# Cross attention after self attention: the order of projection tiles, peaks, scores and the last turn in the second norm, and the order of work at the program's entry

## The reference, cut to what matters

```python
x = x + attention(layer_norm(x, g1, b1), layer_norm(x, g1, b1), wq1, wk1, wv1, wo1, bo1)
x = x + attention(layer_norm(x, g2, b2), context, wq2, wk2, wv2, wo2, bo2)
x = x + geglu_ff(layer_norm(x, g3, b3), w_ff1, b_ff1, w_ff2, b_ff2)
# attention: softmax(q k^T / 8) v per head, then @ wo + bo
# layer_norm: (x - mean) * rsqrt(var + 1e-5) * g + b
```

## Time and profile before

| | us |
|---|---|
| median of 3 runs | 2185.67 |
| lowest and highest | 2182.62 and 2186.26 |
| the profiled execution, its own time | 2181.03 |
| its span, first to last instruction | 2179.3 |

### The profile page before, as it was taken

The page is one execution under the profiler, slowest core; times in us unless marked ns, Lnnn a source line. Parts: engine busy times, 40 slices in busy tenths (PEclk is TensorE's granted clock), DMA queues, the critical chain, the costliest instruction groups (busy, mean ns, idle before and its releaser), DMA issues.

```text
span 2179.3 us, 58920 instructions
## 1 busy us (share of the span) xinstructions
PE 2087.8 (96%) x25120; PEld 1411.8 (65%) x25120; DVE 1622.4 (74%) x3014; ACT 1474.3 (68%) x1950; POOL 1379.3 (63%) x860
## 2 busy tenths in 40 slices
PE   5999999899999999989999999999999999999999
PEld 2666666675666666667466666676746666667675
DVE  5888887557588888665768888866576888885664
ACT  3888889245488888834548888873355888886342
POOL 5878887263378887725347887863434888775450
PEclk8999999999999999999999999999999999999999
DMA  4322320031332232004032233100403323210030
GB/s 129 82 57 64 73 71 19 11 72 49 76 91 65 58 87 53 29 6 99 25 93 74 64 78 75 45 29 6 99 18 93 84 69 84 55 38 21 18 67 20
DMA packets 134245, 127.82 MB, mean 59 GB/s; under 512 B 83424, under 2 KB 95712, under 8 KB 133984
## 3 DMA queue, kind: packets, MB, share of 16 engines
q1 hardware_dynamic: 133744, 123.67, 22.4%
q10 hardware_dynamic: 240, 0.39, 0.1%
HBM read 55.72 MB, written 4.19 MB: 27 GB/s over the span
## 4 chain that ended last, share of the span: by engine, by line
PE 75%; DVE 9%; ACT 5%; POOL 5%; issue 3%; DMA 1%; POOLq 1%; SPq 1%; DVEq 0%; ACTq 0%
PE work L976 10%; PE scores L1000 9%; PE scores L993 9%; PE scores L890 6%; PE scores L892 5%; PE scores L891 5%; PE work L1022 5%; PE work L1018 5%; PE work L1020 5%; PE work L890 4%; PE work L892 4%; PE work L891 4%; DVE minima L1564 2%; ACT prob L1364 1%; PE work L1030 1%
## 5 line engine op out<-in xcount | busy, mean ns | idle before, releaser
L826 POOL TENSOR_TENSOR prob<-prob 128x1024 f16<-128x1024 f32 x328 | 709.0, 2178 | 297.6 <-ACT prob L1364 281.6
L1564 DVE TENSOR_REDUCE minima<-work 128x1 f32<-128x512 f32 x1024 | 681.8, 684 | 53.6 <-PE work L976 47.8
L1363 ACT ACTIVATE prob<-scores 128x1024 f32<-128x1024 f32 x512 | 526.4, 1028 | 93.6 <-PE scores L1000 73.9
L1364 ACT ACTIVATE prob<-scores 128x1024 f16<-128x1024 f32 x512 | 522.8, 1021 | 0.0
L1018 PE MATMUL work<-vals,prob 128*128 128x65 f16 x4096 | 428.8, 192 | 2.2 <-POOL prob L826 1.8
L1022 PE MATMUL work<-vals,prob 128*128 128x65 f16 x4096 | 429.5, 195 | 0.0
L1020 PE MATMUL work<-vals,prob 128*128 128x64 f16 x4096 | 429.2, 193 | 0.0
L1018 PEld LDWEIGHTS work<-vals,prob 128*128 128x128 f16 x4096 | 383.0, 99 | 66.1 <-issue 17.9
L976 PE MATMUL work<-ka,qa 128*128 128x512 f16 x1024 | 390.0, 384 | 28.1 <-DVE minima L1564 19.2
L1020 PEld LDWEIGHTS work<-vals,prob 128*128 128x128 f16 x4096 | 379.8, 97 | 52.8
L1022 PEld LDWEIGHTS work<-vals,prob 128*128 128x128 f16 x4096 | 380.2, 97 | 0.0
(11 more groups left out here) (168 smaller groups left out, 4169.3 us busy)
## 6 DMA issues: line engine op xcount, KB each, us to landing
qa<-staged_q SPq DMA_DIRECT2D x128, 128.0 KB, 2.3
ka<-staged_k SPq DMA_DIRECT2D x126, 128.0 KB, 2.3
raw_even<-in_pairs SPq DMA_DIRECT2D x32, 384.0 KB, 3.4
raw_odd<-in_pairs SPq DMA_DIRECT2D x32, 384.0 KB, 3.4
raw_odd<-in_pieces SPq DMA_DIRECT2D x20, 512.0 KB, 3.3
raw_even<-in_pieces SPq DMA_DIRECT2D x20, 512.0 KB, 3.5
qb<-staged_q SPq DMA_DIRECT2D x64, 128.0 KB, 2.3
kb<-staged_k SPq DMA_DIRECT2D x63, 128.0 KB, 2.3
```

Of the source, the lines that this page charges most:

```text
L826: pool.tensor_tensor(prob[1][:, slot, :], prob32[:, slot, :], prob[0][:, slot, :], ALU.subtract).then_inc(a.polished, 1)
L1363: act.activation(prob32[:, n % RING, :], source, ACT.Exp)
L1364: act.activation(prob[0][:, n % RING, :], source, ACT.Exp)\
L1564: dve.tensor_reduce(minima[:, t, h:h + 1], out[:, :], AX.X, ALU.max, negate=True)\
```

## The change

In the second norm PE does project 6 right behind project 5, then the six peaks of tiles 0 and 1, project 7, turn 2, the six peaks of tiles 2 and 3, and goes to the scores. Shift 0 stands inside score 0, turn 3 behind score 0. The later peaks are spread over four scores (2, 4, 4, 2, places in `X_LATER_AT`), and shift 1 is beside score 4. DVE's list follows: normalise 2 ahead of the first peaks, moments 3 ahead of the second six, normalise 3 behind all twelve, then shift 0 and split 2; split 3 stands ahead of the first peak of step 2. ACT's and POOL's lists for this stage are unchanged.

At the entry, `attention(0)` on SP begins before the bias rows, S1 and W0 are fetched; these come behind the moves of head 1. ACT issues the key moves of head 0 rather than of head 1. DVE does two moments, two normalises, two moments, the low part of the weights, then normalise 2, split 0, normalise 3 and the other splits.

```diff
+X_LATER_AT = {0: (2, 3), 1: (0, 1, 2, 3), 2: (0, 1, 2, 3), 3: (0, 2)}
+X_LATER_STEPS = max(X_LATER_AT)
...
@@ SP, spread @@
+                    if opening and which == "k":
+                        for part in "qk":
+                            for dest, source in moves(part, step.par, 1):
+                                sp.dma_start(dest, source).then_inc(a.head1_ready, 16)
+                        load_rows(0)
+                        fetch(0, "S", 1)
+                        fetch(0, "W", 0)
+                        return
...
-                    if which == "k" and opening:
-                        for dest, source in moves("q", step.par, 1):
-                            sp.dma_start(dest, source).then_inc(a.head1_ready, 16)
...
-            load_rows(0)
-            fetch(0, "S", 1)
-            fetch(0, "W", 0)
...
@@ PE, cross @@
                 project(index, 5, 0)
-                for p in range(2):
-                    for t in (2 * p, 2 * p + 1):
-                        for group in range(len(PEAK_GROUPS)):
-                            peak(t, group)
-                    project(index, p + 6, 0)
+                project(index, 6, 0)
+                for t in range(2):
+                    for group in range(len(PEAK_GROUPS)):
+                        peak(t, group)
+                project(index, 7, 0)
                 turn(index + 1, 2)
-                shift(0)
-                turn(index + 1, 3)
+                for t in range(2, HALF):
+                    for group in range(len(PEAK_GROUPS)):
+                        peak(t, group)
+                later = iter(X_LATER)
                 for n in range(X_ALL):
                     beside = {}
-                    if n < 3:
-                        beside = {k: (peak, at) for k, at in enumerate(X_LATER[4 * n:4 * n + 4])}
-                    elif n == 3:
+                    if n == 0:
+                        beside[1] = shift, (0,)
+                    elif n == X_LATER_STEPS + 1:
                         beside[0] = shift, (1,)
+                    if n == 1:
+                        turn(index + 1, 3)
+                    for k in X_LATER_AT.get(n, ()):
+                        beside[k] = peak, next(later)
                     score(n, beside)
...
@@ ACT, entry @@
-            for dest, source in moves("k", 0, 1):
-                act.dma_start(dest, source).then_inc(a.head1_ready, 16)
+            for dest, source in moves("k", 0, 0):
+                act.dma_start(dest, source).then_inc(a.head0_ready, 16)
...
@@ DVE, cross @@
                 split(index + 1, 1)
-                for t in range(2):
-                    for group in range(len(PEAK_GROUPS)):
-                        peak(t, group)
                 take_y(index, 6)
                 normalise(index + 1, 2)
-                for t in range(2, HALF):
+                for t in range(2):
                     for group in range(len(PEAK_GROUPS)):
                         peak(t, group)
                 take_y(index, 7)
                 moments_of(index + 1, 3)
+                for t in range(2, HALF):
+                    for group in range(len(PEAK_GROUPS)):
+                        peak(t, group)
+                normalise(index + 1, 3)
                 shift(0)
-                normalise(index + 1, 3)
                 split(index + 1, 2)
-                split(index + 1, 3)
+                later = iter(X_LATER)
                 for n in range(X_ALL):
-                    if n < 3:
-                        for at in X_LATER[4 * n:4 * n + 4]:
-                            peak(*at)
-                    elif n == 3:
+                    for at in X_LATER_AT.get(n, ()):
+                        if n == 2 and at == 0:
+                            split(index + 1, 3)
+                        peak(*next(later))
+                    if n == X_LATER_STEPS + 1:
                         shift(1)
...
@@ DVE, entry @@
-            for p in range(GROUPS):
+            for p in range(2):
                 hold(dve, first_loaded[p], 16)
                 moments(0, p)
...
+            normalise(0, 0)
+            normalise(0, 1)
+            for p in range(2, GROUPS):
+                hold(dve, first_loaded[p], 16)
+                moments(0, p)
+            dve.wait_ge(first_weights, 1)
...
+            normalise(0, 2)
+            split(0, 0)
+            normalise(0, 3)
+            for p in range(1, GROUPS):
+                split(0, p)
```

More of the change, by code:

```diff
@@ L1800, in feed_forward @@
                             ahead(name)
-            for p in range(GROUPS):
+            for p in range(2):
                 hold(dve, first_loaded[p], 16)
                 moments(0, p)
[L1805 to L1817, removed]
+            normalise(0, 0)
[4 more added lines that the diff above has]
+            dve.wait_ge(first_weights, 1)
+            high, low = [wp["S"][:, part, :, :].rearrange("p s n -> p (s n)") for part in range(2)]
+            dve.scalar_tensor_tensor(out=low, in0=raw[0][:, 0:6 * P], scalar=W_SCALE, in1=high,
+                                     op0=ALU.mult, op1=ALU.subtract).then_inc(raw_used[0], 1)
+            dve.drain().then_inc(self_split, 1)
+            normalise(0, 2)
[3 more added lines that the diff above has]
+                split(0, p)
             hold(dve, params_loaded, 16)
```

## The result

| | before | changed |
|---|---|---|
| median, us (first comparison, 4 runs each) | 2185.48 | 2159.39 |
| lowest and highest | 2182.62, 2186.26 | 2157.23, 2162.83 |
| ratio, 95% interval | | 0.9883 [0.9872, 0.9895] |
| the profiled execution, its own time | 2181.03 | 2162.83 |
| its span | 2179.3 | 2161.1 |

The changed kernel is 26.1 us faster by the medians; 2163.4 had been forecast. The two profiled executions differ by only 18.2 us: that of before was among the fastest of its kernel and that of the changed kernel the slowest of its four. Why is a point of its own further down.

A forecast was written before the change was run, and what follows sets the result against it. TensorE's own work plus its gaps was taken as the bound. 18.0 us from four rounds and 4.3 from the entry gave 22.3, so 2158.7 against the profiled 2181.03 and a median of 2163.4; range 2154 to 2174.

The forecast's parts named there:

- What bounds the kernel: Whole kernel: TensorE, busy in 96% of the span, sets the length by its own work plus its gaps.
- Part 1: New order in each of four rounds: TensorE's waits fall from 8.7 to 4.2 us, gaining 4.5 per round, 18.0 in four.
- Exponential 0 behind norm 3: ScalarE in each round: norm 3 now precedes exponential 0, done at 422.65; score 2 wants to start at 423.56; cost nothing.
- slower rival: In the rounds, VectorE reaching normalise 3 over 3.7 us late adds time; slower from 9.3 us of lateness; chance 0.04.
- Part 2: Program entry, once: first maximum 6.8 us earlier, but 2.3 us of new wait for S1's split; gain 4.3 us.
- the 28.1 of the shared engines: Entry: time in us when eight key moves in line from 23.8 are through, at 0.54 us each on shared DMA engines.
- the 27.2 of issue time alone: Entry: earliest start of the maxima, in us, if only the issue time of the key moves counted.
- The clock: Entry: TensorE's clock may stay full after a shorter pause; value taken 0, bound +1.2 us.
- The total: Whole kernel: 18.0 from the rounds plus 4.3 from the entry, 22.3 us; forecast median 2163.4.
- S1 does not gate the entry: Rival at the entry: no gating by S1 and the clock stays full; entry gain 8.0, 2159.7 us; chance 0.14.
- Half was not given back: Rival in the rounds: half given back, waits of 6.5 and gain 2.2 per round; 2172.5 us; chance 0.16.
- Nothing gained: Rival: turn waits return at the shift inside score 0 and S1 undoes the entry's key moves; about 2185 us; chance 0.04.

## Why the prediction was right, point by point

- *What bounds the kernel.* PE's work and its gaps. Right: the work stayed (2087.8 and 2087.5 us), and the gaps removed by the change showed in the end.
- *Part 1, the laid-out order.* 4.5 us a round had been worked out; 4.63 was measured. The waits came at the places named: before peaks 5 and 11 (0.45 and 0.43 laid out, 0.36 and 0.35 listed), the shift (0.45, 0.23), the second later peak (0.35, 0.16), and the one that got worse, in score 2 (0.95, 0.82). Score 0's closing pair is 6.2 us earlier against projection 5, as said (15.82 against 22.06).
- *Exponential 0 behind norm 3.* It was said to cost nothing, with 0.9 us of slack. ACT in the changed kernel, the end of norm 3 and the two exponentials of score 0:

```profile
417.92 0.57 ACT L1392 ACTIVATE t<-work,params 128x256 f32<-128x256 f32 x1
418.37 1.03 ACT L1423 ACTIVATE prob<-scores 124x1024 f32<-124x1024 f32 x1
419.27 1.04 ACT L1424 ACTIVATE prob<-scores 124x1024 f16<-124x1024 f32 x1
```

  They end at 420.31, and score 2 starts at 421.37 right behind score 1, with no wait: 1.06 us of slack. The slower rival's condition was never near.
- *Part 2, the entry.* The mechanism was right, S1's fetch behind the moves, with PE waiting for POOL's split behind the ninth maximum. Its size was not: 4.3 had been forecast and 2.1 came. Three terms fell short. The nine moves went out at 0.70 us each rather than 0.645, so S1 was issued at 29.58 and not 29.0. S1 reached POOL after 5.2 us and not 4.0. The 4.0 was taken from a fetch at the head of the line; this one had the rows ahead of it. With both the projections start at 38.26, 2.5 us earlier than before (40.79) instead of 4.3. The third term is the clock, below. The first maximum, at 28.94 and not 28.0 because the last key move took 4.0 us to land and not 3.1, cost nothing, as S1 came later. Window 26 to 28 us of the changed kernel:

```profile
26.00:28.00 2.00, 0.00 (x0) 0.00 (x0) 1.29 (x2) 0.91 (x2) 0.55 (x1) 1.00 1.02 264
```

  The DMA engines are full from 26 to 34 us. The moves' latency was taken from a stretch with one queue at work, though the share of 0.81 for three moves alone stood in the rows. The rule of the Trainium skill (Trainium Kernel Development and Optimization, Key Constraints), that queues of several engines share the same 16 DMA engines, bears on this row. The trace agrees: the key moves that ACT issues beside SP's land after 2.5, 3.8 and 4.0 us, where before, with SP silent, they took 2.2 to 2.4. The first maximum came 0.8 us after the 28.1 of the shared engines and 1.7 after the 27.2 of issue time alone.
- *The clock.* It was taken as 0 at the entry, with a bound of +1.2. It fell at 29.1 in the changed kernel and at 30.7 before, for 13.65 us in both, and the second pair's projections ran at half clock in both. But half clock lasted 4.5 us beyond the start of these projections in the changed kernel and 3.5 before, and over this the lead fell from 2.5 to 2.1 us: a loss of 0.5. Left out altogether was that a round's wait of 2.53 us can bring a half-clock stretch with it, differently in each execution. The trace of before had shown one behind such a wait, at 1491 us, and another at 1550 us behind the wait of 1.94 at the end of the cross stage, which the change does not remove.
- *The total.* Two terms were missing from the sum, the clock in the second norm (1 to 2 us) and the shorter wait at the end of the cross stage (about 1.5). They made up for the entry's shortfall of 2.2. That the forecast of 22.3 us lies so near the measured 23.6 and 24.2 is in this part luck; the 18.0 of the rounds is not (18.5).
- *Rivals.* That S1 does not gate the entry is excluded; it gated more than thought. Half was not given back, since the lead is kept. Nothing gained, and slower, did not come either.

## What to carry to other kernels

Where every engine works in a written order, lay the measured durations along the new order of all engines, not of the busiest alone: the gain of a round came out within 3%. When work is moved past a queue, count every transfer that now stands ahead of the next one needed, also a small one that nobody awaits: here the bias rows made nearly two thirds of the wait for the weights. And a gap on TensorE can cost more than its length, since the clock may be at half behind it; compare executions by their granted clock before a difference of a few microseconds is explained.

## What the runs showed of the hardware

- The granted TensorE clock fell to half for 3.4 or 6.8 us around the end of waits of 1.5 to 2.5 us, in some executions and rounds and not in others of the same program. Over dense work 3.4 us of it cost 1.7 us; where TensorE waited for VectorE soon after, 0 to 0.5 us. The time of a run went with its mean clock: for the kernel before a span of 2180.2 us at 0.997 and of 2187.3 at 0.991.
- A copy of 128 KB within the chip's memory landed 2.3 us after its issue where one queue issued with idle engines, and 2.5 to 4.0 us where two queues issued and the windows show the engines full. POOL could use a 384 KB fetch 3.6 us after its issue with nine such copies ahead of it, and after 5.2 with another 384 KB between.
